# Nested conditional pairs, register loads ahead of them, and the last tile's down product moved, in a routed mixture-of-experts kernel

## What is computed

```python
scores = softmax(xt @ router_w + router_b) + router_bias      # 16 experts, 4 groups
# keep 2 of 4 groups, then the top 2 experts; gate = their scores
for each expert e:
    h = silu(xt @ ew1[e] + eb1[e]) * (xt @ ew2[e] + eb2[e])   # 512 -> 128
    y += gate[:, e] * (h @ ew3[e] + eb3[e])                   # 128 -> 512
z = silu(xt @ sw1 + sb1) * (xt @ sw2 + sb2) @ sw3 + sb3       # shared, 512 -> 256 -> 512
out = x + y + z
```

## Time and profile before

| what | us |
|---|---|
| median of 3 runs | 258.35 |
| the three runs | 254.38, 258.35, 259.02 |
| the profiled execution, its own time | 256.43 |
| its span, first to last instruction | 254.7 |
| PE busy | 233.7 (92%) |
| DVE busy | 131.8 (52%) |
| POOL busy | 111.3 (44%) |
| ACT busy | 81.5 (32%) |
| mean granted PE clock | 0.966 of full |

### The profile page before, as it was taken

The page is one execution under the profiler, slowest core; times in us unless marked ns, Lnnn a source line. Parts: engine busy times, 40 slices in busy tenths (PEclk is TensorE's granted clock), DMA queues, the critical chain, the costliest instruction groups (busy, mean ns, idle before and its releaser), DMA issues.

```text
span 254.7 us, 3970 instructions
## 1 busy us (share of the span) xinstructions
PE 233.7 (92%) x1126; PEld 152.7 (60%) x1127; DVE 131.8 (52%) x266; ACT 81.5 (32%) x177; POOL 111.3 (44%) x136
## 2 busy tenths in 40 slices
PE   4959897999998899999999999999999699999695
PEld 4936544788744467677777777777777244444241
DVE  1294952199998873333333333333333101598982
ACT  1322787231490003333333333333333111111400
POOL 6177455900203554666656666666643310000720
PEclk9985999799999999999999999999999889999979
DMA  7999999999098389545544454555542205999753
GB/s 195 273 289 321 415 414 419 410 423 367 40 373 368 86 249 364 171 165 165 165 153 144 152 159 133 165 165 165 165 165 84 90 0 221 393 388 387 300 200 129
DMA packets 21930, 60.03 MB, mean 236 GB/s; under 512 B 2613, under 2 KB 2741, under 8 KB 21660
## 3 DMA queue, kind: packets, MB, share of 16 engines
q1 hardware_dynamic: 15164, 39.93, 42.3%
q0 software_dynamic: 5600, 17.83, 21.7%
q10 hardware_dynamic: 1152, 2.10, 2.9%
HBM read 43.07 MB, written 17.30 MB: 237 GB/s over the span
## 4 chain that ended last, share of the span: by engine, by line
PE 67%; DVE 20%; DMA 5%; issue 4%; ACT 2%; DVEq 0%; ACTq 0%
PE psum L559 57%; DVE late_region L990 6%; PE psum L735 6%; DMA xt_rows<-r 3%; PE psum L605 3%; DVE xT L1276 3%; DMA xT<-cond_pack 2%; DVE xT L990 2%; PE psum L748 2%; DVE r L990 1%; DVE x_early L990 1%; DVE mixed_w L1027 1%; ACT r L839 1%; DVE r L1232 0%; ACT x_split L863 0%
## 5 line engine op out<-in xcount | busy, mean ns | idle before, releaser
L559 PE MATMUL psum<-wexp,r 128*128 x272 | 68.7, 382 | 0.5 <-DVE r L1232 0.3
L559 PEld LDWEIGHTS psum<-wexp,r 128*128 128x128 f32 x272 | 48.3, 190 | 23.7 <-issue 17.7
L990 DVE TENSOR_TENSOR r<-psum,ebias 128x256 f32<-128x256 f32 x34 | 14.4, 424 | 65.2 <-PE psum L559 65.2
L508 POOL DMA_INDIRECT expert_rows<-late_region,to_row x33 | 33.4, 1011 | 33.3 <-ACT late_region L933 30.3
L498 POOL DMA_INDIRECT late_region<-xt_rows,from_row x36 | 35.3, 980 | 17.9 <-issue 8.8
L559 PE MATMUL psum<-wexp,xt_sb 128*128 x68 | 34.8, 594 | 0.0
L559 PE MATMUL psum<-xT,shared_sb 128*128 128x512 f32 x64 | 29.7, 621 | 2.5 <-issue 2.5
L927 ACT ACTIVATE r<-r 128x128 f32<-128x128 f32 x34 | 10.5, 309 | 55.6 <-DVE r L990 55.6
L933 ACT ACTIVATE late_region<-psum 128x512 f32<-128x512 f32 x34 | 20.3, 597 | 16.1 <-PE psum L559 16.1
L1232 DVE COPY r<-psum 128x512 f32<-128x512 f32 x36 | 24.5, 680 | 0.0
L559 PE MATMUL psum<-x_split,w_split 128*128 128x512 f32 x96 | 23.8, 409 | 0.3 <-DVE logits L990 0.3
(11 more groups left out here) (191 smaller groups left out, 291.3 us busy)
## 6 DMA issues: line engine op xcount, KB each, us to landing
wexp<-expert_pack SPq DMA_DIRECT2D x16, 768.0 KB, 9.4
wexp<-expert_rows SPq DMA_DIRECT2D x8, 1024.0 KB, 12.9
xt_rows<-xt_sb SPq DMA_DIRECT2D x8, 256.0 KB, 8.5
xt_rows<-r SPq DMA_DIRECT2D x8, 256.0 KB, 8.8
x_early<-x SPq DMA_DIRECT2D x1, 2048.0 KB, 15.2
ebias<-expert_bias SPq DMA_DIRECT2D x1, 2048.0 KB, 11.4
out_dram<-x_early SPq DMA_DIRECT2D x8, 256.0 KB, 9.7
shared_sb<-shared_pack SPq DMA_DIRECT2D x1, 1536.0 KB, 19.6
```

The lines of the kernel that those rows point to most:

```text
L508: nc.gpsimd.indirect_dma_start(out=y_dram[:, :], out_offset=bass.IndirectOffsetOnAxis(ap=rows.bitcast(U32), axis=0), in_=y_sb[:, slot, :], ...
L559: return nc.tensor.matmul(dst, lhsT, rhs, start=start, stop=stop)
L990: return nc.vector.tensor_tensor(dst, a, b, op)
```

## The change

On PE, ACT and DVE the conditionals for pairs 16, 17 and the rest are put inside each other: whoever finds `pairs > 17` false leaves by one branch, behind all of them. On POOL the eight conditionals are nested the same way. Registers used behind the conditionals are loaded ahead of them: PE's `last_expert`, ACT's `last_freed`. POOL's copy to `to_slot` goes ahead of the closing pairs, only the wait for it stays behind. On PE the last tile's hidden transpose is taken out of `shared_up(2, 0)` and put right behind the conditionals, and its down product goes behind the first product of `shared_up(2, 0)`, not the third. On DVE `add_rows(0)` goes between the two blocks of `shared_hidden(2)`.

```diff
@@ gpsimd
             pairs, tiles = count_of(pool, N_PAIRS), count_of(pool, N_TILES)
+            nc.gpsimd.tensor_copy(to_slot[:, :], to_row[:, bass.ds(tiles - 1, 1)]).then_inc(to_copied, 1)
             closing_pair(SURE - 2)
             closing_pair(SURE - 1)
-            for p in range(SURE, PAIRS):
+
+            def closing_pairs_from(p):
                 with pool.If(pairs > p):
                     closing_pair(p)
+                    if p + 1 < PAIRS:
+                        closing_pairs_from(p + 1)
+
+            closing_pairs_from(SURE)
+            pool.wait_ge(to_copied, 1)
             pool.wait_ge(y_ready, tiles)
-            nc.gpsimd.tensor_copy(to_slot[:, :], to_row[:, bass.ds(tiles - 1, 1)]).then_inc(to_copied, 1)
-            pool.wait_ge(to_copied, 1)
             scatter(to_slot[:, :], 1)
@@ tensor
-            for q in range(2):
-                with pe.If(pairs > SURE + q):
-                    pe_pair(SURE + q, q, 16 * (SURE // 2 + 1 + q))
-            with pe.If(pairs > SURE + 2):
-                with pe.Fori(1, (PAIRS - SURE) // 2) as j:
...
             last_expert = expert_of(tiles - 1)
+            with pe.If(pairs > SURE):
+                pe_pair(SURE, 0, 16 * (SURE // 2 + 1))
+                with pe.If(pairs > SURE + 1):
+                    pe_pair(SURE + 1, 1, 16 * (SURE // 2 + 2))
+                    with pe.If(pairs > SURE + 2):
+                        with pe.Fori(1, (PAIRS - SURE) // 2) as j:
...
+            hidden_transposed(1, tiles)
             pe.wait_ge(xgT_ready, tiles + 2)
-            shared_up(2, 0, between={(0, 1): lambda: hidden_transposed(1, tiles),
-                                     (0, 2): lambda: down(1, last_expert, tiles, tiles_less_2)})
+            shared_up(2, 0, between={(0, 0): lambda: down(1, last_expert, tiles, tiles_less_2)})
@@ scalar (conditionals nested as on PE)
             pairs, tiles = count_of(act, N_PAIRS), count_of(act, N_TILES)
+            last_freed = count_of(act, N_SCATTERED + 2)
...
             hidden_transposed(1, tiles)
-            result(1, 1, tiles, count_of(act, N_SCATTERED + 2))
+            result(1, 1, tiles, last_freed)
@@ vector (conditionals nested as on PE)
-            shared_hidden(2)
+            shared_hidden(2, [0])
             add_rows(0)
+            shared_hidden(2, [1])
             add_rows(1)
```

More of the change, by code:

```diff
@@ L793, in _ @@
                 pe_pair(j * 2 + 1, 1, j * 16 + 32)
-            for q in range(2):
-                with pe.If(pairs > SURE + q):
-                    pe_pair(SURE + q, q, 16 * (SURE // 2 + 1 + q))
-            with pe.If(pairs > SURE + 2):
-                with pe.Fori(1, (PAIRS - SURE) // 2) as j:
[L800 to L803, removed]
-            last_expert = expert_of(tiles - 1)
+            last_expert = expert_of(tiles - 1)
+            with pe.If(pairs > SURE):
[4 more added lines that the diff above has]
+                        with pe.Fori(1, (PAIRS - SURE) // 2) as j:
+                            for q in range(2):
+                                p = j * 2 + SURE + q
+                                with pe.If(pairs > p):
+                                    pe_pair(p, q, j * 16 + 16 * (SURE // 2 + 1 + q))
+            hidden_transposed(1, tiles)
             pe.wait_ge(xgT_ready, tiles + 2)
-            shared_up(2, 0, between={(0, 1): lambda: hidden_transposed(1, tiles),
-                                     (0, 2): lambda: down(1, last_expert, tiles, tiles_less_2)})
+            shared_up(2, 0, between={(0, 0): lambda: down(1, last_expert, tiles, tiles_less_2)})
             shared_up(2, 1)
@@ L956, in _ @@
             pairs, tiles = count_of(act, N_PAIRS), count_of(act, N_TILES)
[L957 to L967, removed]
+            last_freed = count_of(act, N_SCATTERED + 2)
+            turn = 16 * (SURE // 2)
+            with act.If(pairs > SURE):
+                act_pair(SURE, 0, (turn - 16, turn))
+                with act.If(pairs > SURE + 1):
+                    act_pair(SURE + 1, 1, (turn, turn))
+                    with act.If(pairs > SURE + 2):
+                        with act.Fori(1, (PAIRS - SURE) // 2) as j:
+                            for q in range(2):
+                                p = j * 2 + SURE + q
+                                turn = j * 16 + 16 * (SURE // 2)
+                                with act.If(pairs > p):
+                                    act_pair(p, q, (turn - 16 if q == 0 else turn, turn))
             hidden_transposed(1, tiles)
-            result(1, 1, tiles, count_of(act, N_SCATTERED + 2))
+            result(1, 1, tiles, last_freed)
             shared_silu(2)
@@ L1254, in _ @@
             pairs = count_of(dve, N_PAIRS)
[L1255 to L1261, removed]
+            with dve.If(pairs > SURE):
+                dve_pair(SURE)
+                with dve.If(pairs > SURE + 1):
+                    dve_pair(SURE + 1)
+                    with dve.If(pairs > SURE + 2):
+                        with dve.Fori(SURE + 2, PAIRS) as p:
+                            with dve.If(pairs > p):
+                                dve_pair(p)
             def add_rows(g):
```

## The result

After 257.10 us (median of 20 runs, 255.44 to 260.05) against 255.88 before (20 runs, 252.45 to 259.02); ratio 1.011, 95% interval 1.008 to 1.014, so 2.0 to 3.7 us slower. The ratio leaves out executions more than 1.5% above the fastest of their kernel, and so exceeds the difference over all 20 runs of each, which is 1.2 us of median and 1.4 of mean. The forecast was 256.7 against 257.05: the time lies inside its range and within 2%, but a small gain was said where a small loss came.

A forecast was written before the change was run, and what follows sets the result against it. From 190 us PE bounds the kernel, except where DVE's add_rows(2) decides before PE's last 9.69 us. PE's 2.3 us gain, 1.9 given back, left 0.4 off the runs' middle, 257.05: 256.7 us, range 253.6 to 259.8.

The forecast's parts named there:

- pause before pair 16: PE ahead of pair 16: the new load of last_expert, 0.2 of 0.8 us hidden, delays the loop's end by 0.6 us.
- The clock: PE behind the conditionals: gap 1.4 us instead of 2.49, so full clock holds; work takes 3.55 us instead of 5.32.
- The stretch where DVE decides: Tail: add_rows(2) starts 2.3 us earlier, 1.9 given back; PE waits 4 us instead of 2.09; last 9.69 us stay.
- The turns: DVE and POOL alternate in add_rows(2): four operations drawn out instead of two, giving back 1.9 of 2.3 us.
- the branch: PE's far jump over the remaining pairs to the tail: still 2857 ns; one branch for two saves 0.3 us.
- the load's 0.8: PE between the conditionals and the tail: last_expert is no longer loaded there, 0.8 us less.
- the pattern of the tail: add_rows(2): three operations through, four alternating with POOL's adds, then the eighth; PE idle some 4 us before its last 9.7.
- The order of DVE at 0: add_rows(0) between the two hidden blocks: second block still 1.2 us early for PE's shared_up(3, 1), so cost 0.
- between 1.20 and 2.09, nearer to the first: PE's forecast gap of 1.4 us behind the conditionals, between gaps that did not and did lower the clock; it should hold.
- the packet of the earlier trace: Instruction-fetch queue: one packet moving just after the long branch began, read as PE standing until a fetch lands.
- the clock does fall at the seam: Rival, behind PE's conditionals: the clock falls anyway, +1.7 us, 258.7 us; chance 0.22.
- the fetch gone: Rival, PE's far jump: its target happens to be held, another 1.2 us gained, -1.6 in all, 255.4 us; chance 0.10.

The follow-up runs named there:

- second execution: The kernel before, unchanged, profiled once more; this execution took 256.04 us.
- experiment 11: Kernel before, with three unread filler products on PE behind pair 16's body to keep it busy at the seam: 253.44 us, ratio 0.999.
- experiment 1: Changed kernel, with POOL's last adds held back until add_rows(2) is done: 251.59 us, ratio 0.989 to the kernel before.
- experiment 5: Changed kernel, with DVE's order as before (both blocks of shared_hidden(2), then add_rows(0)): 257.18 us, ratio 1.011 to the kernel before.
- experiments 4 and 8: Changed kernel, short jump plus POOL's last adds held back: 249.91 us, 0.985; the same with DVE doing all eight last-group adds: 250.35 us, 0.988.
- experiment 7: Changed kernel, with 17 unread products filling PE's wait between shared_down(2) and shared_down(3): 254.72 us, ratio 1.003 to the kernel before.
- experiments 5 and 2: The first has its own line; the second: kernel before, with POOL's last adds held back until add_rows(2) is done: 254.65 us, ratio 0.999.
- third execution: The kernel before, unchanged, in another profiled execution; this one took 255.67 us.
- experiment 6: Changed kernel, with the load of last_expert put back behind the conditionals: 259.44 us, ratio 1.021 to the kernel before.

## Why the prediction was wrong, step by step

The forecast in the terms of the table, us, and what came:

```
                                forecast                  measured (averages)
                          before  after  change       before  after  change
pause before pair 16         0     0.6    +0.6           0     0.5    +0.5
to add_rows(2)             34.3   31.4    -2.9         33.6   32.6    -1.0
from there                 21.3   23.2    +1.9         19.9   23.1    +3.2
sum                                       -0.4                        +2.7
```

*The step that failed* is the clock, in two places. In "The clock", the fall at the seam was taken as what the kernel before always pays, and 1.8 us credited in full; in the second execution it held behind a gap of 2.18 us. In "The stretch where DVE decides", PE "falls to half clock as before. The last 9.69 us stay": they were 9.69 in the one execution of the earlier trace rows and 8.00 in the two others and in experiment 11. What was written down as unchanged is for most executions a new cost of 1.7 us. The turns, written down as DVE giving back 1.9 of 2.3, cost just that, but there were not 2.3 us to give back: the way to `add_rows(2)` became 1.0 us shorter on average. The sum then moved to the middle of the runs, 257.05 (20 runs put the median at 255.88), but it kept a difference made from one execution, in which both falls were there. The forecast even said "4 us instead of 2.09" and asked nothing more of it.

*A term mis-sized:* the branch, 3628 ns for the 2857 taken over, so the gap was 2.01 us for 1.4; the longer branch took back most of the load's 0.8. It explains 0.6 of the 0.7 us by which the profiled execution of after missed the forecast. In five traces of before that branch took 2457 to 3002 ns, in five of after with its far jump 2767 to 3628, and 2061 in experiment 1. One row was no measure of it.

*Right, by the trace of after:* the pattern of the tail, with three operations through, four in turns and PE idle for 3.97 us (4). The pause before pair 16 was 0.5 us (0.6). The order of DVE at 0: experiment 5. Counted from the loop's last product, each event came 0.8 to 0.9 us later than said: the last scatter at 5.7 (4.8), the loads at 8.5 (7.7), POOL's adds at 33.7 (32.9), PE at the end of `shared_up(3, 1)` at 30.8 (30.0). In the time of the trace the same events lie within 0.4 us of the forecast (204.23 for 204.5, 207.10 for 207.4, 232.23 for 232.6, 229.38 for 229.7), but that is luck: this execution reached the closing pairs 1.1 us earlier, with a granted clock of 0.97 in its first 60 us for 0.91 in before.

*No argument:* that the clock held behind 2.01 us and fell behind 1.83 in experiment 5 says that "between 1.20 and 2.09, nearer to the first" could not tell. That it held in the profiled execution of after was luck too. And the packet of the earlier trace rows was no sign by itself that the branch waits for it.

*The rivals:* the clock does fall at the seam in some executions of after, for 1.3 us (2.1 said); the fetch gone is worth 2.1 us against after (1.2 said against the forecast), but takes an edit of the loop. The rival that was missing is the one that happened: the wait made longer brings a fall of its own.

*Open:* in which executions the clock falls at the seam. The same program did both, and three traces on a side give no shares. How often before falls in the tail is known from four traces only, once. Executions also differ by falls in the first 60 us, in code that no edit touches (granted clock 0.97 there in after, 0.91 in before, 0.86 in the second execution of before); they moved the loop's end in before from 199.14 to 202.45 us and can hide a difference of 3 us in the tail. Why the packet of instructions moves when it does, and what takes 2.4 us and more behind it, is not shown.

## What to carry to other kernels

Before a stall of one profiled execution is credited or called unchanged, take two more profiles of the same kernel: what depends on the granted clock may be there in one and not in the next. Compare two executions from a common point in the work, not by the time since the start. Rows that are ready sooner are no gain by themselves: ask which engine will use them sooner, and beside whom. Where two engines take turns, start the one that nobody waits for behind the other, by a wait if need be: one line, 4.5 us in the tail of the changed kernel, but nothing clear of noise in the kernel before.

## What the runs showed of the hardware

A taken compare-and-branch over far code took 2061 to 3628 ns in eleven traces, ending 2.4 to 2.9 us behind a packet of the instruction queue, and 341 to 349 ns in the three with the short jump; not taken, at the entry of pair 16, it was 67 to 75. An operation of DVE of 0.69 us (5.51 for eight) takes up to 1.78 beside an add of POOL, and the two engines in turns did not get more done than DVE alone (5.5 us both, experiments 4 and 8). The Trainium skill (SBUF — State Buffer, "SBUF: two separate sides") describes the two as excluding each other, and these rows agree. Behind PE's idle time in the tail the clock fell in all five traces with 3.94 to 4.04 us, and in one of four with 1.07 to 2.09 us. At the seam it held behind 1.69, 2.01 and 2.18 us (experiment 7, after, the second execution of before) and fell behind 1.83, 2.09, 2.49 and 2.75 (experiments 5 and 2, before, its third execution), and behind 1.15 and 0.66 us with a transpose between them (experiment 6). So the length alone does not tell it, but the longest wait was never free. Seventeen products of no use in that wait saved 2.0 to 2.4 us.
